# Gated attention and feed-forward kernel: another order of loads, maxima and row sums in the prologue

## What is computed

```python
def _ws(w):                                   # weight standardization, row by row
    m = w.mean(axis=1, keepdims=True)
    v = w.var(axis=1, keepdims=True)
    return (w - m) * jax.lax.rsqrt(v + EPS)
def _conv(x, w, b, mask):
    return (jnp.einsum('oc,bct->bot', _ws(w), x) + b[None, :, None]) * mask
# attention, on xn = _layernorm(x): q and k from y, v from xn; 8 heads of 32
q, k, v = _conv(y, wq, bq, mask_cond), _conv(y, wk, bk, mask_cond), _conv(xn, wv, bv, mask)
scores = jax.nn.softmax(jnp.einsum('bhdt,bhet->bhde', q, k) / SCALE, axis=-1)
out = _conv(einsum('bhde,bhet->bhdt', scores, v), wo, bo, mask) + xn
x = x + jnp.tanh(g_xattn[0]) * (normalize(out) * gamma + beta) * mask
# feed-forward on xr = _layernorm(x), 4096 rows of 1024
gates = top_2_of_8(softmax(xr @ wr.T))
h = silu(silu(xr @ w1.T) @ w3.T) @ w2.T
x = x + jnp.tanh(g_ffn[0]) * scatter_add(gates * h)   # into rows 0 to 7
```

## Time and profile before

| | us |
|---|---|
| median of 3 runs | 1243.17 (1241.69 to 1245.37) |
| the profiled execution | 1245.78, its span 1244.0 |
| TensorE busy | 1102.8 (89%) |
| VectorE busy | 842.8 (68%) |
| ScalarE busy | 466.9 (38%) |
| GpSimd busy | 387.2 (31%) |
| DMA | 65.8 MB, mean 53 GB/s |

### The profile page before, as it was taken

The page is one execution under the profiler, slowest core; times in us unless marked ns, Lnnn a source line. Parts: engine busy times, 40 slices in busy tenths (PEclk is TensorE's granted clock), DMA queues, the critical chain, the costliest instruction groups (busy, mean ns, idle before and its releaser), DMA issues.

```text
span 1244.0 us, 18398 instructions
## 1 busy us (share of the span) xinstructions
PE 1102.8 (89%) x6871; PEld 646.5 (52%) x6871; DVE 842.8 (68%) x1951; ACT 466.9 (38%) x762; POOL 387.2 (31%) x404
## 2 busy tenths in 40 slices
PE   1656699899989999899989999899989999799998
PEld 1445455655556546554556546554556546555553
DVE  4589567975696758865696757875696757864322
ACT  3662434234234524244234524244234524234231
POOL 2281012550255113550255113550255113540000
PEclk9977699999999999899999999899999999899999
DMA  9601300041001500041001500041001500023000
GB/s 271 169 18 73 114 1 1 2 142 62 1 1 35 170 2 1 1 150 55 1 1 34 170 2 1 1 148 57 1 1 34 170 2 1 1 86 138 1 1 1
DMA packets 35214, 65.78 MB, mean 53 GB/s; under 512 B 1758, under 2 KB 19748, under 8 KB 35132
## 3 DMA queue, kind: packets, MB, share of 16 engines
q1 hardware_dynamic: 33660, 63.25, 15.8%
q10 hardware_dynamic: 1472, 1.31, 0.4%
HBM read 47.75 MB, written 16.81 MB: 52 GB/s over the span
## 4 chain that ended last, share of the span: by engine, by line
PE 42%; DVE 34%; ACT 10%; issue 9%; POOL 3%; DMA 1%; ACTq 0%; DVEq 0%; POOLq 0%
PE bank L608 26%; PE bank L479 6%; DVE ub L1067 5%; DVE act_t L1180 3%; DVE ub L1086 3%; ACT h_hi L815 3%; DVE xbuf L1109 3%; DVE h_lo L1185 3%; DVE ub L1082 2%; ACT ub L786 2%; DVE xt_lo L1161 2%; PE bank L533 2%; PE bank L488 2%; DVE bst L1103 2%; DVE bst L1022 2%
## 5 line engine op out<-in xcount | busy, mean ns | idle before, releaser
L608 PE MATMUL bank<-xt_hi,w1b 128*128 128x512 f16 x1024 | 328.2, 381 | 20.4 <-DVE xt_lo L1161 14.1
L608 PE MATMUL bank<-w3b,h_hi 128*128 128x512 f16 x1024 | 310.3, 385 | 2.8 <-DVE act_t L1180 2.8
L608 PE MATMUL bank<-w3b,h_lo 128*128 128x512 f16 x512 | 196.2, 383 | 0.0
L608 PE MATMUL bank<-xt_lo,w1b 128*128 128x512 f16 x512 | 195.1, 381 | 0.0
L1185 DVE SCALAR_TENSOR_TENSOR h_lo<-act_t,h_hi 128x512 f16<-128x512 f32 x128 | 125.7, 982 | 91.5 <-ACT h_hi L815 91.5
L1180 DVE SCALAR_TENSOR_TENSOR act_t<-act_t,bank 128x512 f32<-128x512 f32 x128 | 85.9, 671 | 133.5 <-ACT act_t L809 133.2
L809 ACT ACTIVATE act_t<-bank,fs 128x512 f32<-128x512 f32 x128 | 87.4, 683 | 234.4 <-PE bank L608 234.4
L608 PEld LDWEIGHTS bank<-xt_hi,w1b 128*128 128x128 f16 x1024 | 100.4, 98 | 135.0 <-DVE xt_lo L1161 13.6
L815 ACT ACTIVATE h_hi<-act_t 128x512 f16<-128x512 f32 x128 | 80.6, 630 | 219.7 <-DVE act_t L1180 219.7
L608 PEld LDWEIGHTS bank<-w3b,h_hi 128*128 128x128 f16 x1024 | 100.6, 99 | 73.8 <-DVE act_t L1180 4.2
L393 POOL TENSOR_TENSOR ub<-bo_b,mcur 128x2048 f32<-128x2048 f32 x16 | 57.6, 3600 | 202.2 <-DVE dg L1044 202.2
(11 more groups left out here) (189 smaller groups left out, 1946.6 us busy)
## 6 DMA issues: line engine op xcount, KB each, us to landing
xbuf<-in_x_dram SPq DMA_DIRECT2D x16, 1024.0 KB, 5.8
out_dram<-xbuf SPq DMA_DIRECT2D x16, 1024.0 KB, 4.7
x_lo<-in_ctx_dram SPq DMA_DIRECT2D x16, 512.0 KB, 5.9
mrow<-in_mask_dram SPq DMA_DIRECT2D x16, 512.0 KB, 4.5
w1b<-in_w_dram SPq DMA_DIRECT2D x8, 512.0 KB, 7.5
w3b<-in_w_dram SPq DMA_DIRECT2D x8, 512.0 KB, 7.4
xbuf<-in_w_dram SPq DMA_DIRECT2D x1, 4096.0 KB, 13.6
ub<-in_wq_dram ACTq DMA_DIRECT2D x1, 256.0 KB
```

Of the source, the lines that this page charges most:

```text
L608: mm = pe.matmul(bk[:, :], left, right, start=d == 0 and n == 0, stop=d == FT - 1 and n == 2)
```

## The change

Nothing of what is computed changes, only order and place:

- The four matrices get a semaphore of their own (`wn_in`), so `small_in` counts 11 loads. SP issues y first, then x, then the small arrays. wr lands in another buffer (`wrf`, in `h1_lo`).
- VectorE begins with the matrices' statistics (`weights_ready`, with one more small memset), then the maxima of y, then `ln1`. `prepare` is taken apart: `qk_low`, `y_scale`, `mask_tables`, then `y_low`, then `biases`; the low parts of bv and wr move to `small_low`, after stage 1.
- GpSimd makes the matrices' coefficients first, then y's all-reduce (two columns), then `ln1` twice. The small maxima have an all-reduce of their own in stage 0, w1's is in stage 3, ahead of the second bias tile and behind both `add_beta`, w3's in stage 9.
- w1's row sums are made after stages 0 (two of eight), 1 (three) and 2 (three); their maximum (`row_largest`) after stage 2, the scale after stage 3. w1 is transposed, copied and split in stages 4, 5, 6 and 9 instead of 3 to 6. w3's row maximum is taken after stage 8.
- ScalarE normalizes x and makes the tanh behind the high parts of y; the high parts of bv and wr move to stage 1. TensorE transposes masks and wr behind the matrices, and waits for the low parts of wv and bv only ahead of `times_value`.

```diff
-SMALL = 16 * 15
-W1_TR = range(3, 7)
+SMALL = 16 * 11
+W1_TR = (4, 5, 6, 9)
...
+        wrf = h1_lo[0:NE, 0:4, :].rearrange("p a n -> p (a n)").bitcast(F32)
...
+        mats = [(wn[:, 2 * n:2 * n + 2, :], a[w].rearrange("(c p) n -> p c n", p=P))
+                for n, w in enumerate(("wq", "wk", "wv", "wo"))]
+        smalls = [(wrf, a["wr"]), (msk, a["mask"].rearrange("q o (t p) -> (q o t) p", p=P)),
...
-            load_x(0)
-            for dst, src in smalls[8:]:
-                sp.dma_start(dst, src).then_inc(sm["small_in"], 16)
             for b in range(2):
                 sp.dma_start(ya[b], yd[b]).then_inc(y_in[b], 16)
+            load_x(0)
+            for dst, src in smalls[4:]:
+                sp.dma_start(dst, src).then_inc(sm["small_in"], 16)
             load_mask(0)
             sp.wait_ge(sm["small_in"], SMALL)
...
-            def y_largest(j, n):
+            def y_largest(j):
 
                 pool.wait_ge(sm["y_max"], 2 * j + 2)
                 pool.tensor_tensor(pspare[:, :], minus[:, 0:1], minus[:, 0:1], ALU.mult)
-                pool.partition_all_reduce(ms[:, 1, 0:n], ms[:, 0, 0:n], P, RMAX).then_inc(sm["y_all"], 1)
+                pool.partition_all_reduce(ms[:, 1, 0:2], ms[:, 0, 0:2], P, RMAX).then_inc(sm["y_all"], 1)
+
+            def small_largest():
+
+                pool.wait_ge(sm["w_max"], 1)
+                pool.partition_all_reduce(ms[:, 1, 2:4], ms[:, 0, 2:4], P, RMAX).then_inc(sm["w_all"], 1)
...
             def attention(j, s, jn=None):
-                if s == 1 and first_pair(j):
+                if s == 0 and first_pair(j):
+                    small_largest()
+                if s == 3 and first_pair(j):
                     largest(1, 0)
+                if s == 9 and first_pair(j):
+                    largest(2, 1)
                 if s == 12 and jn is not None:
-                    y_largest(jn, 2)
+                    y_largest(jn)
                 if s in (3, 4) and not first_pair(j):
                     ln1(2 * j + s - 3)
                 if s in (2, 3):
@@ -411,14 +421,12 @@
                     b, q = s - 10, 2 * j + s - 10
                     coefs(q, mv2, co2, CH, EPS, XS, "ln2", (sm["xs2_ready"], q))
 
+            coefs(0, mvc, coc, 8, EPS, 1.0, "ws", None)
+            y_largest(0)
             ln1(0)
             ln1(1)
-            coefs(0, mvc, coc, 8, EPS, 1.0, "ws", None)
-            pool.wait_ge(sm["w_max"], 1)
-            y_largest(0, 4)
             for s in range(STAGES):
                 attention(0, s, 1)
-            largest(2, 1)
...
                 pe.wait_ge(sm["ident_set"], 1)
-                pe.wait_ge(sm["small_in"], SMALL)
-                pe.transpose(fbk[0][:, 0:P], msk, ident[:, :])
-                pe.transpose(fbk[0][:, P:P + NB * CT], mskc, ident[0:NB * CT, 0:NB * CT])
...
                     last.then_inc(sm["ws_tr"], 1)
+
+                pe.wait_ge(sm["small_in"], SMALL)
+                pe.transpose(fbk[0][:, 0:P], msk, ident[:, :])
+                pe.transpose(fbk[0][:, P:P + NB * CT], mskc, ident[0:NB * CT, 0:NB * CT])
...
-                pe.wait_ge(sm["wv_lo_set"], 1)
-                pe.wait_ge(sm["bv_lo_set"], 1)
...
             def times_value(q, b):
 
+                if first_pair(q):
+                    pe.wait_ge(sm["wv_lo_set"], 1)
+                    pe.wait_ge(sm["bv_lo_set"], 1)
...
-            for dst, src in smalls[:8]:
+            for dst, src in mats:
+                act.dma_start(dst, src).then_inc(sm["wn_in"], 16)
+            for dst, src in smalls[:4]:
                 act.dma_start(dst, src).then_inc(sm["small_in"], 16)
-            for b in range(2):
-                normed(b, b, co, sm["ln1_coef"], sm["xs_ready"])
-            act.wait_ge(sm["small_in"], SMALL)
-            act.activation(tg[:, :], graw, ACT.Tanh).then_inc(sm["tg_set"], 1)
-
             act.wait_ge(sm["ws_coef"], 1)
...
-            act.wait_ge(sm["w_scale"], 1)
-            act.wait_ge(sm["bias_set"], 1)
-            act.activation(bv_hi[:, :, :], bv_b[:, :, :], ACT.Copy, scale=sc[:, 3, 2:3]).then_inc(sm["bv_hi_set"], 1)
...
-            def row_sums(k):
+            def small_high():
+
+                act.wait_ge(sm["w_scale"], 1)
+                act.wait_ge(sm["bias_set"], 1)
+                act.activation(bv_hi[:, :, :], bv_b[:, :, :], ACT.Copy, scale=sc[:, 3, 2:3]).then_inc(sm["bv_hi_set"], 1)
+                act.wait_ge(sm["wr_tr"], 1)
+                act.activation(wr_t[:, :, 0:NE], fbk[1][:, 0:FT * NE].rearrange("p (d n) -> p d n", d=FT), ACT.Copy,
+                               scale=sc[:, 2, 2:3]).then_inc(sm["wr_hi"], 1)
+
+            def row_sums(k, fs_):
 
                 for half in "ab":
                     act.wait_ge(sm[f"w{1 + 2 * k}{half}_in"], 64)
-                for f in range(FT):
+                for f in fs_:
...
-            row_sums(0)
+            act.wait_ge(sm["small_in"], SMALL)
+            act.activation(tg[:, :], graw, ACT.Tanh).then_inc(sm["tg_set"], 1)
+            for b in range(2):
+                normed(b, b, co, sm["ln1_coef"], sm["xs_ready"])
...
+                if s == 0:
+                    row_sums(0, range(0, 2))
+                if s == 1:
+                    small_high()
+                    row_sums(0, range(2, 5))
+                if s == 2:
+                    row_sums(0, range(5, FT))
                 if s == 6:
-                    row_sums(1)
+                    row_sums(1, range(FT))
...
-            def scale_of(n, k):
-
-                dve.tensor_reduce(sc[:, k, 0:1], wsum[:, k, :], AX.X, ALU.max,
-                                  apply_absolute_value=True).then_inc(sm["w_max"], 1)
-                dve.wait_ge(sm["w_all"], n)
-                powers(n, slice(k, k + 1), sc[:, k, 1:2])
-
-            def prepare():
-                dve.wait_ge(sm["small_in"], SMALL)
-
+            def weights_ready():
+
+                dve.wait_ge(sm["sc_zero"], 1)
+                dve.wait_ge(sm["wn_in"], 64)
                 for n in range(8):
...
                 dve.wait_ge(sm["ws_stat"], 1)
+                carry()
                 for n in range(8):
                     ins = dve.bn_aggr(mvc[:, n, :], bst2[:, n, :])
                 ins.then_inc(sm["ws_mv"], 1)
+
+            def qk_low():
+                for n in range(2):
+                    dve.wait_ge(sm["ws_copy"], n + 1)
+                    dve.scalar_tensor_tensor(out=wqk_lo[:, n, :], in0=att[n][:, :], scalar=WS, in1=wqk_hi[:, n, :],
+                                             op0=ALU.mult, op1=ALU.subtract).then_inc(sm["ws_lo"], 1)
+
+            def mask_tables():
...
+            def biases():
...
-                dve.wait_ge(sm["bias_set"], 1)
                 dve.wait_ge(sm["sc_zero"], 1)
-
-                dve.tensor_reduce(ms[0:NE, 0, 2:3], wrs, AX.X, ALU.max, apply_absolute_value=True)
+                dve.tensor_reduce(ms[0:NE, 0, 2:3], wrf, AX.X, ALU.max, apply_absolute_value=True)
                 dve.tensor_reduce(ms[:, 0, 3:4], vcol[:, 0:CH], AX.X, ALU.max, apply_absolute_value=True)\
                     .then_inc(sm["w_max"], 1)
-                for b in range(2):
-                    y_largest(0, b)
-                for n in range(2):
-                    dve.wait_ge(sm["ws_copy"], n + 1)
-                    dve.scalar_tensor_tensor(out=wqk_lo[:, n, :], in0=att[n][:, :], scalar=WS, in1=wqk_hi[:, n, :],
-                                             op0=ALU.mult, op1=ALU.subtract).then_inc(sm["ws_lo"], 1)
                 dve.wait_ge(sm["wv_hi_set"], 1)
                 dve.scalar_tensor_tensor(out=wv_lo[:, :, :], in0=ws[:, 4:6, :], scalar=WS, in1=wv_hi[:, :, :],
                                          op0=ALU.mult, op1=ALU.subtract).then_inc(sm["wv_lo_set"], 1)
-                y_scale(0)
+
+            def small_low():
+
+                dve.wait_ge(sm["w_all"], 1)
                 powers(0, slice(2, 4), ms[:, 1, 2:4])
...
+            def row_largest(k):
+                dve.wait_ge(sm["w_rows"], FT * (k + 1))
+                dve.tensor_reduce(sc[:, k, 0:1], wsum[:, k, :], AX.X, ALU.max,
+                                  apply_absolute_value=True).then_inc(sm["w_max"], 1)
+
             def weight_scale(k):
-                dve.wait_ge(sm["w_rows"], FT * (k + 1))
-                scale_of(1 + k, k)
+                dve.wait_ge(sm["w_all"], k + 2)
+                powers(k + 1, slice(k, k + 1), sc[:, k, 1:2])
                 scales(k)
...
+            weights_ready()
+            for b in range(2):
+                y_largest(0, b)
             ln1(0, 0)
             ln1(0, 1)
-            prepare()
+            qk_low()
+            y_scale(0)
+            mask_tables()
             for b in range(2):
                 y_low(0, b)
             masks(0)
+            biases()
             for s in range(STAGES):
                 if s in W1_TR:
                     for i in range(4):
-                        weight(4 * (s - W1_TR[0]) + i)
```

(39 more changed lines are left out.)

## The result

The changed kernel takes 1268.97 us (median, 1267.96 to 1269.72) against 1243.58 for the kernel before, 1.020 times as long (95% interval 1.0186 to 1.0221). The forecast was 1257.2, with a range of 1249 to 1265. The direction and the kind of cause held; the loss was larger than the range allowed.

The account below looks back on a forecast made before the run. The kernel's change was taken to equal that of the first feed-forward product's start, set by prologue waits. 10.4 us ahead of attention_out plus 3.6 at the prologue's end made 14.0: 1259.8 profiled, 1257.2 as median; range 1249 to 1265.

Parts of the forecast that it names:

- Maximum of y: Prologue, y's first all-reduce: over at 27.0 us instead of 35.1, y_low at 29.2, a 9.0 us gain for the first projection.
- ln1: Behind y's all-reduce: load back of 7.1 us, then two coefficient sets, done at 37.25; 2 of the 9 us lost.
- What bounds the kernel, and where the change acts: Only the part before the first feed-forward product (146.73 us) changes; the later part repeats behind TensorE.
- Code loads and their number: GpSimd visits all-reduce code five times instead of two; each load there 6.45 to 7.45 us, back 7.1, delaying queued work.
- The prediction's side estimate for loads of 5.95 us each: Were every GpSimd code load 5.95 us, the sum would be an estimated 9 us instead of 14.
- Loads: Start of the prologue, memory loads: matrices land at 13.8 us instead of 19.04, x with them, y near 7.5.
- Maximum of w1: w1's all-reduce, queued behind the beta additions (done at 74.75): ready at 81.6 us, before at 48.15.
- Restart: From w1's maximum to attention_out: cb done at 85.8, x_low from 92.3, overlap with bias_tiles as before; attention_out 10.4 us late.
- End of the prologue: From second coefficients through w3's maximum, ln2 and y's next all-reduce: ACT's y_high 3.1 to 4.1 us late, taken as 3.6.
- that loads are hidden: Rival: GpSimd code loads finish before their instructions may start; 8.7 us less, 1234.5; chance 11%.
- that only the way to the all-reduce costs: Rival: loads back cost nothing; w1's maximum at 67.4, total 1239.3, mixed cases 1240 to 1247; chance 7%.
- The matrices did come sooner: Answers the rival that queues don't take turns by packet and matrices land at 19: 1262; no separate chance given.

Follow-up runs that it names:

- Experiment 4: The kernel before with one GpSimd all-reduce of a constant column, awaited by nobody, added after stage 8's coefficients: 1250.55 us against 1243.09.
- experiment 1: The changed kernel with VectorE's ln1 statistics of example 1 moved behind the bias steps, after the matrices' low parts and y's scale: 1263.60 us.
- experiment 5: The changed kernel with example 1's ln1 behind VectorE's bias steps, small maxima beside w1's and w3's maximum beside y's, so three all-reduce visits: 1245.94 us.
- experiment 9: A two-visit kernel keeping the change's good parts, prologue end reordered, with example 1's beta additions held until both bias tiles' sums: 1223.57 us, 0.9837 of the kernel before.

## Why the prediction was wrong

The step that failed is in the terms "Maximum of y" and "ln1". They put at nothing a wait of VectorE inside `ln1`, for the load back on GpSimd, and what is queued behind it on VectorE and ScalarE. The runs showed this wait to be 12.4 us long on VectorE and the second ln1 coefficients to be 10.0 us later than forecast, 8.0 of them by this chain.

- **What bounds the kernel, and where the change acts: right.** The part behind the first product kept its length (1097.3 and 1095.8 us).
- **Code loads and their number: right.** Five visits; loads of 5.8 to 7.7 us, priced at 6.45 to 7.45, and 6.9 to 7.5 back, priced at 7.1. Experiment 4 shows the price of a visit at one place alone, 7.5 us. (The prediction's side estimate for loads of 5.95 us each is off: worked through, its sum gives some 7 us, not 9, since it has 4.4 us less of loads ahead of attention_out and 2.7 less behind.)
- **Loads: nearly right.** The matrices landed at 14.56, forecast 13.8.
- **"Maximum of y": wrong in its second half.** The all-reduce was over at 28.7 (forecast 27.0), but y_low was to follow at 29.2 and came at 41.17. The prediction names `qk_low` and `y_scale` nowhere, though the change puts them behind `ln1` on VectorE. `ln1` of example 1 waits for GpSimd's coefficients of example 0, and so for the load back. Before, that wait was over at once; the change moved what it waits for behind a code load. VectorE stood 12.4 us there, and y's scale paid 10.8 of them (39.24, against 28.44 in experiment 1).
- **"ln1": the term that failed most.** 37.25 was forecast for the second coefficients, 47.2 was measured. 2.0 of the 10 are the later matrices and two loads of 7.66 and 7.50 us. The other 8.0 are this chain: ScalarE's normalization of example 0 is queued behind the high parts of y (39.9 to 42.1), it ends at 44.5, and the second coefficients wait for it. In experiment 1 the second coefficients are ready at 41.9, 5.4 earlier; the rest is that ScalarE can't start before the first coefficients (2.55 us in GpSimd's rows there).
- **"Maximum of w1": right from there on.** The steps are as forecast. From the second coefficients to the maximum I had 44.4 us; 42.8 were measured. Its place, 90.1 instead of 81.6, is 8.5 late, all inherited.
- **"Restart": right by luck.** cb done at 94.0, 3.9 us after the maximum (forecast 4.2). attention_out started 18.45 late instead of 10.4. I had assumed that x_low and bias_tiles would overlap as before, and they nearly did (9.57 against 10.94). That was luck: the experiments show that this term can be 3.2 or 14.2, so it should have stood among the bounds, and as a rival of its own.
- **"End of the prologue": small.** 3.6 forecast, 5.1 measured (166.07 less 142.53 and 18.45). The same kind of wait again: ln2's second coefficients wait for ScalarE (2.55 us in GpSimd's list), not for the load.
- **Range: too narrow on the slow side.** It held mis-sized loads but no wait that was left out. 8.0 us more ahead of attention_out and 1.5 us more behind it carry the forecast to 1266.7. The other 2.2 us are between profile and median: the forecast took 2.6 off, as far as the profiled execution of before lay above its median, and that of after lies on its median.
- **Rivals:** that loads are hidden, and that only the way to the all-reduce costs, are both refuted by GpSimd's list (all nine stand there, four of them behind an all-reduce). The matrices did come sooner.

Closed: the three edits of experiment 5 undo 23.0 of the 25.4 us, of which 4.7 are relief from a collision that the kernel before had too. Open: what the visit still added costs by itself in that kernel. Not tried: whether a load can be hidden by placing its first instruction ahead of a wait.

## What to carry to other kernels

A GpSimd all-reduce cost its queue some 13 us here when ordinary arithmetic stands on both sides, not 0.4: put all-reduces side by side, even if some of them then come later than they could. When a step moves behind a long stall, list not only who waits for it but every wait inside the steps of the other engines that refers back to it, and what is queued behind those; a buffer with one copy makes such a wait in the writer. And before making an engine arrive earlier, look at what GpSimd is doing at that moment: the kernel of experiment 9, put in order by these points, is 1.6% faster than the kernel before, and the kernel before with two waits added is 0.4% faster than without.

## What was not expected of the hardware

- The eight sums of `bias_tiles` took 3.25 us beside an idle GpSimd, and 14.18, 10.94, 9.57, 4.59 and 3.95 us in other kernels, the longer the more of GpSimd's work fell on them (0.7 to 0.9 us for each us of overlap).
- A visit to an all-reduce whose result nobody reads took 13.2 us of GpSimd's queue (5.89 + 0.38 + 6.95) and 7.5 us of the kernel.
- The way back costs as much as the way there, also when it follows at once (in the changed kernel 6.88 to 7.50 us after an all-reduce of 0.4 us).
